# A tuned two-layer network kernel: leaking unit inside the MLP's products, shorter root chain, vector index from its known score, rounding in one piece

## Chip, cores and metric

One core of a Trainium2 chip. The metric is the device time in microseconds, the median of the runs. Engines: TensorE (PE, its weight loads PEld), VectorE (DVE), ScalarE (ACT), GpSimd (POOL), SyncE (SP, DMA issue).

## The reference

The input is `x` of 16 x 96 x 96 x 96 (images, channels, height, width). Two layers, each a mixing part and a feed-forward part with residuals:

```python
# layer 0
x = x + _L0_conv_ref(_ln_c(x), ...)
t = t + _L0_ffn_ref(_ln_t(t), W1, b1, W2, b2)      # t: x as tokens
# layer 1
x = x + _L1_conv_ref(_ln_c(x))                      # x / (2 + 1e-4 * 5x5 sum of squares) ** 0.75
t = t + _L1_ffn_ref(_ln_t(t), W1, b1, W2, b2)
```

The mixing part of layer 0 works on patches of 3 x 3 pixels. Each pixel is compared with 512 vectors; the best pair of pixel and vector is found, and an MLP makes the patch from it:

```python
y = einsum('ncij,vc->nvij', patches, w_mask) / (x_norm * w_norm)
idx = argmax(y.reshape(NL, -1))                     # max_ch, max_col = idx // 9, idx % 9
integrate = max_act * max_sim + w_mask[max_ch] * (1.0 - max_sim)
inp = concatenate([integrate, sim_map_max])         # 96 + 9
h = leaky_relu(inp @ w_i1.T + b_i1, 0.2)            # 288
vcs = tanh(h @ w_i2.T + b_i2)
h1 = relu(vcs @ w_l1.T + b_l1)
h2 = h1 @ w_l2.T + b_l2                             # then w_conv
```

The feed-forward parts (96 to 384 to 96) round their inputs, weights and hidden values to an 8-bit float (5 exponent, 2 mantissa bits) and sums to 16 bits.

## The kernel before

A tile is 128 patches (partitions) of J = 9 pixels and C = 96 channels; there are 128 tiles, 8 per image (`SLOTS`). The program is a software pipeline written by hand: each engine runs `steps(body)`, and in step k every part works on another tile (`PARTS`: `fs` loads and statistics, `f1` scores and selection, `f2` the search of the vector, `f3` the MLP, `back` and `tail` the feed-forward of layer 0, `pre` and `rear` layer 1). There are 145 steps; in the last ones only layer 1 is left. Engines run their bodies in the written order and wait for each other by semaphores, so the order of each body sets the order of the work.

What the change and the prediction touch, by the order in a step:

- Scores, TensorE `score` (L375, product L385) and VectorE `score_max` (L728, L731): nine 128x512 products go into two banks in turn, and VectorE takes the maximum over the 512 vectors of each (`mx`). Product j waits for maximum j-2 (`score_taken`).
- `mlp_input` (L778) on VectorE makes `inp` (96 + 9 columns) for the MLP. The links of `pixel_roots` (L707, `inverse_root` L688) go between: a seed by integer arithmetic (L692), the input times -0.5 (L693), then three rounds of three links (L697, L700, L703), each waiting for the one before by a semaphore, and the last instruction `nb1` (L717), which sets `root_ready`. GpSimd begins its step behind `root_ready` (L1067).
- The MLP: TensorE turns `inp` (L402), ScalarE copies it (`inpT`), `mlp_in` (L407) makes three 96x128 products, ScalarE adds the bias to each (`z1`, L596), VectorE makes the leaking unit in one instruction (`leaky`, L799: the larger of z and 0.2 z), and `mlp_mid` (L414) sums three products. Then tanh (L606), `mlp_last` (L420), `conv` (L428), `residual1` (L807).
- The vector: the chosen pixel (`win`, gathered by GpSimd, L968) is turned (L391), multiplied with all 512 vectors again (`win_scores`, L397), and `win_vector` (L768) takes the largest score (MAX8, L772) and its index (L775), with which GpSimd gathers the vector (`wrow`, L976) and multiplies it with the tile (L984, L986).
- `hidden` (L812) on VectorE: for each of three 128x1152 blocks of hidden values an addition of the bias with relu (L817), and a rounding to 8-bit precision on the 16-bit pattern (L823), once per block, in two pieces of a chain: block c is rounded after the addition of block c+1. `fill` on TensorE waits for all three (`hid_ready`, L367), then makes 27 products (L370). Links of other chains go between, by `run(between, 1)`.
- `select` (L736): similarity, its maximum and index, the row number `xrow` for the pixel's gather, a cast of the index to float (`jf`, L753), a mask of the nine columns (`pick`, L756), and two products with the mask that sum (L759, L761).
- `lrn_columns` (L835): once per image, a chain on 128x72 values with another `inverse_root`, its links between other instructions of two steps. The step that has most of it is called the LRN step here; it follows the step with the window sums (`window_sums`, L432). GpSimd's `keep_root2` waits for its end (`lrn_ready`) in that step.
- `moments` (L947) on GpSimd makes the roots' arguments from the statistics (`args_ready`); `gather_pixel` stands behind it.

```python
                scores(0, 2)
                if k.f3 is not None:
                    leaky(k.f3)
                scores(2, WIN_TURN)
                if k.fs is not None:
                    dve.wait_ge(xt_loaded[k.p], landed(k.fs, k.p))
                    last = group_stats(1, xt[:, k.fs & XT - 1], between)
                if k.f2 is not None:
                    win_vector(k.f2, between)
```

## Time and profile before

| | |
|---|---|
| median of 3 runs | 3665.52 us (3658.46 to 3670.87) |
| the profiled execution: time, span | 3659.15 us, 3657.4 us |
| instructions | 63346 |
| VectorE busy | 3093.2 us (85%), 11127 instructions |
| TensorE busy | 3038.1 us (83%), 17928 instructions |
| ScalarE busy | 2890.6 us (79%), 7558 instructions |
| GpSimd busy | 2569.9 us (70%), 3993 instructions |
| HBM | 52 GB/s over the span |
| mean granted TensorE clock | 0.945 |

Busy time is the union of an engine's instructions; records of one engine overlap a little. Idle time stands before the instruction that ended it, with the engine and the instruction that released it. The granted clock is a share of 2.4 GHz.

### The profile page before, as it was taken

Reading aid. Unit: us, or ns where it says so; the run is one execution under the profiler, and the core shown is the slowest. Engines: PE = TensorE matmul, PEld = TensorE weight load, DVE = VectorE, ACT = ScalarE, POOL = GpSimd, SP = SyncE. Lnnn points to the kernel's source line nnn. Section 1 sums busy time; section 2 is a strip of 40 time slices with the busy share of each in tenths; the row PEclk is TensorE's granted clock in tenths of the full one; section 3 lists DMA queues with packets and bytes.
Section 4 is the critical chain, followed back from the end, with each engine's and each line's share of the span. In section 5 each row is a group of like instructions: output and inputs, shape, how many; then the busy total and the mean of one; then the engine's idle time right before and its main releaser. Section 6 shows DMA issues by size and latency. Waiting matters only on the chain. (4 is left out here: it accounts for less than half of the span.)

```text
span 3657.4 us, 63346 instructions
## 1 busy us (share of the span) xinstructions
PE 3038.1 (83%) x17928; PEld 1674.1 (46%) x17928; DVE 3093.2 (85%) x11127; ACT 2890.6 (79%) x7558; POOL 2569.9 (70%) x3993
## 2 busy tenths in 40 slices
PE   5887888888888888888888888888888888888755
PEld 2444454444445444444444444444444444444332
DVE  6788989889888998889889888889998888999631
ACT  0444888878788887878878788888888888888877
POOL 2455677767777777777767777776777777777753
PEclk9999999999999999999999999999999999999855
DMA  3111111111111121111111111121211111111000
GB/s 84 45 37 45 46 60 54 60 50 56 58 55 60 50 65 50 57 58 55 60 50 57 58 55 55 55 65 50 60 55 56 59 50 61 54 59 46 23 30 34
DMA packets 64515, 195.70 MB, mean 54 GB/s; under 512 B 11392, under 2 KB 14633, under 8 KB 64169
## 3 DMA queue, kind: packets, MB, share of 16 engines
q1 hardware_dynamic: 53928, 172.76, 14.8%
q0 software_dynamic: 10240, 18.89, 2.1%
q8 instruction: 148, 2.42, 0.3%
q14 instruction: 199, 1.62, 0.1%
HBM read 134.60 MB, written 57.02 MB: 52 GB/s over the span
## 5 line engine op out<-in xcount | busy, mean ns | idle before, releaser
L385 PE MATMUL banks<-wcT,xc 128*128 128x512 f32 x2304 | 1217.4, 631 | 108.8 <-DVE mx L731 104.2
L518 ACT ACTIVATE ffn_hid<-banks 128x384 f16<-128x384 f32 x2304 | 1026.8, 487 | 296.5 <-PE banks L362 273.1
L731 DVE TENSOR_REDUCE mx<-banks 128x1 f32<-128x512 f32 x1152 | 774.7, 683 | 227.9 <-PE banks L385 218.4
L362 PE MATMUL banks<-ffn_xT,w1q 128*128 128x384 bf16 x2304 | 678.1, 348 | 177.4 <-ACT ffn_hid L518 138.3
L994 POOL TENSOR_TENSOR ffn_f<-ffn_y,b2q 128x864 f16<-128x864 f16 x256 | 469.7, 1835 | 375.5 <-DVE nb L717 300.1
L362 PEld LDWEIGHTS banks<-ffn_xT,w1q 128*128 128x128 bf16 x2304 | 228.7, 100 | 790.6 <-ACT ffn_hid L518 588.1
L385 PEld LDWEIGHTS banks<-wcT,xc 128*128 128x128 f32 x2304 | 422.6, 199 | 350.8 <-DVE mx L731 150.8
L817 DVE TENSOR_SCALAR ffn_hid<-ffn_hid,b1q 128x1152 f16<-128x1152 f16 x768 | 420.9, 559 | 126.1 <-ACT ffn_hid L518 126.0
L996 POOL TENSOR_TENSOR x<-x,ffn_f 128x864 f32<-128x864 f32 x256 | 488.3, 1907 | 20.1
L551 ACT ACTIVATE ffn_x<-x,cols 128x96 fp8e5<-128x96 f32 x1152 | 461.4, 456 | 0.0
L551 ACT ACTIVATE ffn_x<-x,nb,roots 128x96 fp8e5<-128x96 f32 x1152 | 424.9, 455 | 0.0
L724 DVE BATCH_NORM_STATS2 st<-x 128x6 f32<-128x96 f32 x2304 | 408.0, 245 | 8.9 <-POOL x L996 8.9
L984 POOL TENSOR_TENSOR prod_dot<-xt,wrow 128x864 f32<-128x864 f32 x128 | 271.0, 2117 | 200.3 <-DMA wrow<-vector_table,vidx 200.3
L428 PE MATMUL banks<-wc,h 128*128 128x480 f32 (+1 forms) x1024 | 393.2, 527 | 0.0
L518 ACT ACTIVATE ffn_xT<-banks 96x384 bf16<-96x384 f32 x768 | 345.1, 483 | 60.0 <-PE banks L355 40.2
L370 PEld LDWEIGHTS banks<-w2q,ffn_hid 128*128 128x128 f16 x6912 | 330.1, 101 | 127.2 <-issue 125.2
L518 ACT ACTIVATE ffn_y<-banks 128x480 f16<-128x480 f32 (+1 forms) x512 | 257.1, 531 | 163.4 <-PE banks L370 146.9
L370 PE MATMUL banks<-w2q,ffn_hid 128*128 128x96 bf16 x6912 | 351.8, 211 | 39.2 <-DVE ffn_hid L823 39.2
L355 PE MATMUL banks<-ident_b,ffn_x 128*96 128x128 bf16 x2304 | 228.1, 227 | 144.3 <-ACT ffn_xT L518 116.9
L823 DVE TENSOR_SCALAR ffn_hid<-ffn_hid 128x1152 uint16<-128x1152 uint16 x768 | 338.3, 452 | 0.0
L355 PEld LDWEIGHTS banks<-ident_b,ffn_x 128*96 128x96 fp8e5 x2304 | 177.9, 125 | 255.1 <-ACT ffn_xT L518 155.7
L564 ACT ACTIVATE x<-x,cols 128x96 f32<-128x96 f32 x640 | 293.3, 460 | 0.3 <-POOL cols L1004 0.3
(147 smaller groups left out, 4474.0 us busy)
## 6 DMA issues: line engine op xcount, KB each, us to landing
xt<-x_tok_in SPq DMA_DIRECT2D x128, 432.0 KB, 3.2
xc<-x_chan_in SPq DMA_DIRECT2D x128, 432.0 KB, 3.6
out_tok<-x SPq DMA_DIRECT2D x128, 432.0 KB, 2.5
win<-x_tok_in,xrow POOLq DMA_INDIRECT x128, 2.6
wrow<-vector_table,vidx POOLq DMA_INDIRECT x128, 2.7
shift<-shift_in SPq DMA_DIRECT2D x1, 960.0 KB, 5.7
vector_table<-wtab SPq DMA_DIRECT2D x1, 384.0 KB, 3.3
...
```

The lines of the kernel that those rows point to most:

```text
L355: last = pe.matmul(bank[0:C, i * P:(i + 1) * P], ffn.x8[:, u * G + i, :], ident_b[:, :], start=True, stop=True)
L362: last = pe.matmul(bank[:, 0:GW], w1q[:, ffn.layer, c * P:(c + 1) * P], ffn.xT[:, g * GW:(g + 1) * GW], start=True, stop=True)
L370: last = pe.matmul(bank[:, (j - j0) * C:(j - j0 + 1) * C], ffn.hid[:, c, j * P:(j + 1) * P], w2q[:, ffn.layer, c, :], start=(c == 0), stop ...
L385: last = pe.matmul(ps_score[score_bank(j)], xc[p][:, j, :], wcT[:, :], start=True, stop=True)
L428: last = pe.matmul(bank[:, 0:(j1 - j0) * C], h1[:, q, :], wc[:, q, j0 * C:j1 * C], start=(q == 0), stop=(q == 1))
L518: return nc.scalar.activation(dst, src, ACT.Copy)
L551: last = nc.scalar.activation(ffn.x8[:, j, :], x[:, j, :], ACT.Identity, bias=bias_c[:, j:j + 1], scale=scale_c[:, j:j + 1], saturate=False)
L724: last = nc.vector.bn_stats(st3[:, which, j, :], src[:, j, :])
L731: nc.vector.tensor_reduce(mx[p][:, j:j + 1], ps_score[score_bank(j)], AX.X, ALU.max).then_inc(score_taken, 1)
L817: nc.vector.tensor_scalar(ffn.hid[:, c, :], ffn.hid[:, c, :], b1q[:, ffn.layer, c:c + 1], 0.0, ALU.add, ALU.max).then_inc(ffn.rounded, 1)
L994: tt(ffn.f[:, :, :], ffn.y[:, :, :], b2, ALU.add).then_inc(ffn.f_ready, 1)
L996: tt(dst, x, ffn.f[:, :, :], ALU.add).then_inc(ready, 1)
```

## The change

1. The leaking unit is written as 0.2 z + 0.8 relu(z). The linear part, with the bias, goes through a matrix made once at the start (`leak`, from `wi1r` and `wi2`, times 0.2), as a fourth product of `mlp_mid` on `inpT`. `inp` gets a 106th column of ones, which carries the bias `b_i1`. ScalarE makes 0.8 relu(z) of all three blocks in one instruction, straight into `h`. `z1`, `z1_ready` and VectorE's `leaky` go.
2. `inverse_root` has a seed and seven links: one round with a polynomial of second degree (four links), one of Newton's (three). The multiplication by -0.5 beside the seed goes, since the factor sits in the first link of a round.
3. `select` compares `iota` with the index directly, without the cast, and a third product with the mask writes the raw score of the chosen pixel into `vtop`. `win_vector` looks for that score at once; its MAX8 and one link go.
4. `hidden` adds to all three blocks first and then rounds 128x3456 in one instruction; `hid_ready` is set once per tile.

```diff
@@ mlp_mid
                 pe.wait_ge(h_ready, f3 + 1)
+                pe.matmul(ps_a[0:C, 0:P], leak[:, :], inpT[:, :], start=True, stop=False)
                 for c in range(M1):
-                    last = pe.matmul(ps_a[0:C, 0:P], wi2[:, c, :], h[:, c, :], start=(c == 0), stop=(c == M1 - 1))
+                    last = pe.matmul(ps_a[0:C, 0:P], wi2[:, c, :], h[:, c, :], start=False, stop=(c == M1 - 1))
@@ scalar, body
                     act.wait_ge(z1_made, k.f3 + 1)
-                    for c in range(M1):
-                        last = nc.scalar.activation(z1[:, c * P:(c + 1) * P], ps_b[0:C, c * P:(c + 1) * P],
-                                                    ACT.Identity, bias=bmlp[:, c:c + 1])
-                    last.then_inc(z1_ready, 1)
+                    nc.scalar.activation(h[:].rearrange("c m p -> c (m p)"), ps_b[0:C, 0:M1 * P], ACT.Relu,
+                                         scale=1.0 - LEAK).then_inc(h_ready, 1)
@@ vector
-            root_links = 11
+            root_links = 8
...
-                chain.add(nc.vector.tensor_scalar(y.bitcast(i32), x.bitcast(i32), -0.5, ROOT_SEED, ALU.mult, ALU.add),
-                          nc.vector.tensor_scalar(xh, x, -0.5, None, ALU.mult))
-                yield
-                for _ in range(3):
+                chain.add(nc.vector.tensor_scalar(y.bitcast(i32), x.bitcast(i32), -0.5, ROOT_SEED, ALU.mult, ALU.add))
+                yield
+                for scale, inner, outer in ((ROOT_POLY[2] ** 0.5, ROOT_POLY[1] / ROOT_POLY[2] ** 0.5, ROOT_POLY[0]),
+                                            (-0.5, None, 1.5)):
                     chain.wait()
-                    chain.add(nc.vector.tensor_tensor(t, y, y, ALU.mult))
+                    chain.add(stt(out=t, in0=y, scalar=float(scale), in1=y, op0=ALU.mult, op1=ALU.mult))
                     yield
                     chain.wait()
-                    chain.add(nc.vector.tensor_tensor(t, t, xh, ALU.mult))
+                    chain.add(nc.vector.tensor_tensor(t, t, x, ALU.mult))
                     yield
+                    if inner is not None:
+                        chain.wait()
+                        chain.add(stt(out=t, in0=t, scalar=float(inner), in1=t, op0=ALU.add, op1=ALU.mult))
+                        yield
                     chain.wait()
-                    chain.add(nc.vector.scalar_tensor_tensor(out=y, in0=t, scalar=1.5, in1=y, op0=ALU.add,
-                                                             op1=ALU.mult))
+                    chain.add(stt(out=y, in0=t, scalar=float(outer), in1=y, op0=ALU.add, op1=ALU.mult))
                     yield
@@ select
-                f1c.add(nc.vector.tensor_copy(jf[:, :], jidx[:, 0:1]))
-                yield
-                f1c.wait()
-                f1c.add(nc.vector.tensor_scalar(pick[p][:, :], iota[:, :], jf[:, 0:1], None, ALU.is_equal))
+                f1c.add(nc.vector.tensor_tensor(pick[p][:, :], iota[:, :], jidx[:, 0:1].broadcast_to([P, J]),
+                                                ALU.is_equal))
...
+                nc.vector.scalar_tensor_tensor(out=junk[:, 2, :], in0=pick[p][:, :], scalar=1.0, in1=mx[p][:, :],
+                                               op0=ALU.mult, op1=ALU.mult,
+                                               accum_out=vtop[p][:, 0:1]).then_inc(pick_ready, 1)
@@ win_vector
                 dve.wait_ge(win_scored, f2 + 1)
-                f2c.begin(f2)
-                f2c.add(nc.vector.max(vtop[:, :], ps_score[0]))
-                next(between, None)
-                f2c.wait()
-                nc.vector.max_index(vidx[:, :], vtop[:, :], ps_score[0]).then_inc(vidx_ready, 1)
+                dve.wait_ge(pick_ready, f2 + 1)
+                nc.vector.max_index(vidx[:, :], vtop[q][:, :], ps_score[0]).then_inc(vidx_ready, 1)
@@ hidden
-                relu(0)
-                run(between, 1)
-                for c in range(1, HC):
+                for c in range(HC):
                     relu(c)
                     run(between, 1)
-                    round_up(c - 1)
-                    run(between, 1)
-                round_up(HC - 1)
+                dve.wait_ge(ffn.rounded, (tile + 1) * HC)
+                bits = ffn.hid[:, :, :].rearrange("p c n -> p (c n)").bitcast(U16)
+                nc.vector.tensor_scalar(bits, bits, TO_E5M2, TO_E5M2, ALU.add,
+                                        ALU.subtract).then_inc(ffn.hid_ready, 1)
+                run(between, 1)
@@ vector, body
                 scores(0, 2)
-                if k.f3 is not None:
-                    leaky(k.f3)
                 scores(2, WIN_TURN)
```

VectorE's order at the end of a step, where the hidden values of layer 0 are rounded with the selection between (`ffn_hid` the hidden values, `sim` to `junk` the selection). Before, up to the last rounding piece, behind which two products with the mask follow:

```order
L817 TENSOR_SCALAR ffn_hid<-ffn_hid,b1q 128x1152
L741 TENSOR_TENSOR sim<-mx,roots 128x9
L817 TENSOR_SCALAR ffn_hid<-ffn_hid,b1q 128x1152
L744 MAX top<-sim 128x8
L823 TENSOR_SCALAR ffn_hid<-ffn_hid 128x1152
L747 MAX_INDEX jidx<-top,sim 128x8
L817 TENSOR_SCALAR ffn_hid<-ffn_hid,b1q 128x1152
L751 TENSOR_TENSOR xrow<-jidx,row_base 128x1
L753 CAST jf<-jidx 128x1
L823 TENSOR_SCALAR ffn_hid<-ffn_hid 128x1152
L756 TENSOR_SCALAR pick<-iota,jf 128x9
L823 TENSOR_SCALAR ffn_hid<-ffn_hid 128x1152
```

With the change:

```order
L825 TENSOR_SCALAR ffn_hid<-ffn_hid,b1q 128x1152
L755 TENSOR_TENSOR sim<-mx,roots 128x9
L825 TENSOR_SCALAR ffn_hid<-ffn_hid,b1q 128x1152
L758 MAX top<-sim 128x8
L825 TENSOR_SCALAR ffn_hid<-ffn_hid,b1q 128x1152
L761 MAX_INDEX jidx<-top,sim 128x8
L833 TENSOR_SCALAR ffn_hid<-ffn_hid 128x3456
L765 TENSOR_TENSOR xrow<-jidx,row_base 128x1
L767 TENSOR_TENSOR pick<-iota,jidx 128x9
L771 SCALAR_TENSOR_TENSOR junk,wmean<-pick,mom 128x9
L773 SCALAR_TENSOR_TENSOR junk,wrstd<-pick,roots 128x9
L776 SCALAR_TENSOR_TENSOR junk,vtop<-pick,mx 128x9
```

Two of the three rounding instructions are gone and the one left is three times as wide; `xrow` stands behind it, and there is a third product with the mask.

VectorE's order behind the roots (`mx` the score maxima, `h` the leaking unit, `vtop` and `vidx` the search of the vector). Before:

```order
L731 TENSOR_REDUCE mx<-banks 128x1 x2
L799 SCALAR_TENSOR_TENSOR h<-z 96x384
L731 TENSOR_REDUCE mx<-banks 128x1 x2
L724 BN_STATS st<-xt 128x6 x9
L772 MAX vtop<-banks 128x8
L775 MAX_INDEX vidx<-vtop,banks 128x8
L731 TENSOR_REDUCE mx<-banks 128x1
```

With the change:

```order
L745 TENSOR_REDUCE mx<-banks 128x1 x4
L738 BN_STATS st<-xt 128x6 x9
L788 MAX_INDEX vidx<-vtop,banks 128x8
L745 TENSOR_REDUCE mx<-banks 128x1
L738 BN_STATS st<-x 128x6 x9
```

The leaking unit and the MAX are gone, the four maxima stand together.

TensorE's order around the MLP's middle product (`xc` the score products, `h` and `leak` the middle product, `winT` the chosen pixel's scores). Before:

```order
L385 MATMUL banks<-wcT,xc 128x512
L362 MATMUL banks<-ffn_xT,w1q 128x384 x2
L385 MATMUL banks<-wcT,xc 128x512
L414 MATMUL banks<-h,wi 96x128 x3
L362 MATMUL banks<-ffn_xT,w1q 128x384 x2
L420 MATMUL banks<-vcs,wl 72x128 x2
L397 MATMUL banks<-wcT,winT 128x512
```

With the change:

```order
L393 MATMUL banks<-wcT,xc 128x512
L370 MATMUL banks<-ffn_xT,w1q 128x384 x2
L393 MATMUL banks<-wcT,xc 128x512
L421 MATMUL banks<-inpT,leak 96x128
L423 MATMUL banks<-h,wi 96x128 x3
L370 MATMUL banks<-ffn_xT,w1q 128x384 x2
L429 MATMUL banks<-vcs,wl 72x128 x2
L405 MATMUL banks<-wcT,winT 128x512
```

One product on `inpT` is added ahead of the three.

## Rows read from the trace of the kernel before

**Rows 1.** The page's first part: busy time, share and instructions of each engine.

```profile
PE 3038.1 (83%) x17928; PEld 1674.1 (46%) x17928; DVE 3093.2 (85%) x11127; ACT 2890.6 (79%) x7558; POOL 2569.9 (70%) x3993
```

**Rows 2.** Windows: busy us of PE, PEld, DVE, ACT, POOL, granted clock, DMA.

```profile
1000.00:2000.00 1000.00, 861.95 (x5249) 477.19 (x5248) 892.20 (x3226) 844.59 (x2213) 748.65 (x1152) 0.98 0.18 57
...
1753.00:1757.00 4.00, 4.00 (x14) 1.87 (x12) 2.37 (x4) 1.23 (x3) 3.92 (x3) 0.66 0.00 0
```

**Rows 3.** Timeline, VectorE, ordinary step: start us, busy us, line, tiles, [idle before].

```profile
1890.29 0.59 DVE L785 TENSOR_REDUCE dots<-half_dot 128x9 f32<-128x432 f32 x1
...
1891.54 0.18 DVE L692 TENSOR_SCALAR roots<-args 128x36 int32<-128x36 int32 x1
1891.64 0.41 DVE L693 TENSOR_SCALAR rtmp<-args 128x36 f32<-128x36 f32 x1
...
1892.08 0.20 DVE L697 TENSOR_TENSOR rtmp<-roots 128x36 f32<-128x36 f32 x1
...
1894.14 0.17 DVE L717 SCALAR_TENSOR_TENSOR nb<-mom,roots 128x9 f32<-128x9 f32 x1
...
1895.43 1.20 DVE L799 SCALAR_TENSOR_TENSOR h<-z 96x384 f32<-96x384 f32 x1
...
1899.94 0.70 DVE L772 MAX8 vtop<-banks 128x8 f32<-128x512 f32 x1 [0.49 <-PE banks L397]
...
1909.70 0.69 DVE L731 TENSOR_REDUCE mx<-banks 128x1 f32<-128x512 f32 x1 [1.17 <-PE banks L385]
...
1915.64 0.59 DVE L785 TENSOR_REDUCE dots<-half_dot 128x9 f32<-128x432 f32 x1
```

**Rows 4.** Timeline of the same step, TensorE.

```profile
1892.12 0.36 PE L402 MATMUL banks<-ident,inp 128*105 128x128 f32 x1 [0.52 <-DVE inp L794]
...
1894.13 0.31 PE L391 MATMUL banks<-ident,win 128*96 128x128 f32 x1
1894.96 1.13 PE L385 MATMUL banks<-wcT,xc 128*128 128x512 f32 x2 [0.52 <-DVE mx L731]
...
1897.11 0.82 PE L414 MATMUL banks<-h,wi 96*96 96x128 f32 x6
```

**Rows 5.** Timeline of the same step, GpSimd.

```profile
1890.45 0.25 POOL L962 TENSOR_TENSOR args<-var,eps 128x27 f32<-128x27 f32 x1
...
1903.82 1.09 POOL L976 DMA_INDIRECT wrow<-vector_table,vidx  x1
...
1911.92 0.50 POOL L955 TENSOR_TENSOR mtmp<-st 128x27 f32<-128x27 f32 x2 [0.69 <-DVE st L724]
```

**Rows 6.** Groups of instructions, VectorE: the rounding pieces.

```profile
L823 DVE TENSOR_SCALAR ffn_hid<-ffn_hid 128x1152 uint16<-128x1152 uint16 x768 | 338.3, 452 | 0.0
```

**Rows 7.** Timeline of an LRN step: VectorE, then TensorE, then GpSimd.

```profile
1835.01 1.87 DVE L799 SCALAR_TENSOR_TENSOR h<-z 96x384 f32<-96x384 f32 x1 [1.15 <-ACT z L596]
...
1845.19 2.27 DVE L817 TENSOR_SCALAR ffn_hid<-ffn_hid,b1q 128x1152 f16<-128x1152 f16 x1
...
1837.03 0.87 PE L414 MATMUL banks<-h,wi 96*96 96x128 f32 x6 [0.85 <-DVE h L799]
...
1851.77 2.08 PE L385 MATMUL banks<-wcT,xc 128*128 128x512 f32 x2 [3.00 <-DVE mx L731]
...
1845.10 2.05 POOL L984 TENSOR_TENSOR prod_dot<-xt,wrow 128x864 f32<-128x864 f32 x1 [1.77 <-DMA wrow<-vector_table,vidx]
```

**Rows 8.** Timeline of the step behind it, TensorE.

```profile
1865.84 0.45 PE L391 MATMUL banks<-ident,win 128*96 128x128 f32 x1 [1.29 <-DMA win<-x_tok_in,xrow]
```

**Rows 9.** Timeline of a step of the drain, VectorE and TensorE.

```profile
3539.07 0.52 DVE L817 TENSOR_SCALAR ffn_hid<-ffn_hid,b1q 128x1152 f16<-128x1152 f16 x1 [0.87 <-ACT ffn_hid L518]
3539.50 0.82 DVE L823 TENSOR_SCALAR ffn_hid<-ffn_hid 128x1152 uint16<-128x1152 uint16 x2
...
3540.47 2.32 PE L370 MATMUL banks<-w2q,ffn_hid 128*128 128x96 bf16 x27 [1.97 <-DVE ffn_hid L823]
```

More of the change, by code:

```diff
@@ L42 @@
 HC = HID // P
-D1 = C + J
+D1 = C + J + 1
+LEAK = 0.2
 M1 = 3
@@ L61 @@
 ROOT_SEED = float(0x5F3759DF)
+ROOT_POLY = np.polynomial.Chebyshev.interpolate(
+    lambda w: w ** -0.5, 2, domain=[0.9324, 1.0691]).convert(kind=np.polynomial.Polynomial).coef
 LRN_POLY = np.polynomial.Chebyshev.interpolate(
@@ L132, in build @@
         wi2 = sb("wi2", [C, M1, C])
+        wi1r = sb("wi1r", [C, M1, D1])
+        leak = sb("leak", [D1, C])
         wl1 = sb("wl1", [C, 2 * LH])
@@ L136, in build @@
         wc = sb("wc", [P, 2, J * C])
-        bmlp = sb("bmlp", [C, M1 + 1 + 2])
+        bmlp = sb("bmlp", [C, 1 + 2])
         w1raw = sb("w1raw", [C, 2, HID])
@@ L164, in build @@
         roots = [sb(f"roots_{i}", [P, 4, J]) for i in range(2)]
-        rtmp = sb("rtmp", [P, 2, 4 * J])
+        rtmp = sb("rtmp", [P, 4 * J])
         nb1 = sb("nb1", [P, J])
@@ L177, in build @@
         winT = sb("winT", [P, P])
-        vtop = sb("vtop", [P, 8])
+        vtop = [sb(f"vtop_{i}", [P, 8]) for i in range(2)]
         vidx = sb("vidx", [P, 8], U32)
@@ L330, in _ @@
         def _(pe):
-            pe.wait_ge(w_loaded, 16 * 15)
+            pe.wait_ge(w_loaded, 16 * 16)
             pe.wait_ge(table_ready, 1)
@@ L341, in _ @@
                                      wconv[:, :], start=True, stop=True)
+            for c in range(M1):
+                last = pe.matmul(banks[0:D1, 5, 0:C], wi1r[:, c, :], wi2[:, c, :], start=(c == 0), stop=(c == M1 - 1))
             last.then_inc(w_pe, 1)
@@ L527, in _ @@
                 last = copy(wc[0:LH + q, q, 5 * C:J * C], banks[0:LH + q, 2 + 2 * q, 0:4 * C])
-            last.then_inc(w_act, 1)
+            nc.scalar.activation(leak[:, :], banks[0:D1, 5, 0:C], ACT.Copy, scale=LEAK).then_inc(w_act, 1)
             def take(ffn, tile, first, units):
@@ L648, in _ @@
             nc.vector.memset(st3[:], 0.0)
+            for v in vtop:
+                nc.vector.memset(v[:], 0.0)
             nc.vector.memset(h1[:], 1.0)
+            nc.vector.memset(inp[:], 1.0)
             nc.vector.memset(wc[:], 0.0)
@@ L714, in pixel_roots @@
                 y = flat(roots[k.p])
-                yield from inverse_root(rc, flat(args), y, rtmp[:, 0, :], rtmp[:, 1, :])
+                yield from inverse_root(rc, flat(args), y, rtmp[:, :])
                 rc.wait()
@@ L787, in mlp_input @@
                          nc.vector.tensor_scalar(mix[:, 1:2], top_q, -1.0, 1.0, ALU.mult, ALU.add))
-                f3c.add(nc.vector.tensor_tensor(inp[:, C:D1], dots[:, :], roots[q][:, 3, :], ALU.mult),
+                f3c.add(nc.vector.tensor_tensor(inp[:, C:C + J], dots[:, :], roots[q][:, 3, :], ALU.mult),
                         nc.vector.tensor_scalar(wnorm[:, :], win[q][:, :], wmean[q][:, 0:1], mix[:, 0:1],
@@ L795, in mlp_input @@
                                                in1=wnorm[:, :], op0=ALU.mult, op1=ALU.add).then_inc(inp_ready, 1)
-            def leaky(f2):
-                dve.wait_ge(z1_ready, f2 + 1)
-                nc.vector.scalar_tensor_tensor(out=h[:].rearrange("c m p -> c (m p)"), in0=z1[:, :], scalar=0.2,
-                                               in1=z1[:, :], op0=ALU.mult, op1=ALU.max).then_inc(h_ready, 1)
             def residual1(f2, q):
@@ L839, in lrn_columns @@
                 alpha, beta, rstd, bias = (flat(b) for b in cols_i)
-                w, t, rg, arg, xh = (lbuf[:, i, :] for i in range(5))
+                w, t, rg, arg = (lbuf[:, i, :] for i in range(4))
                 dve.wait_ge(box_made, n + 1)
@@ L874, in lrn_columns @@
                 lc.wait()
-                yield from inverse_root(lc, arg, rstd, t, xh)
+                yield from inverse_root(lc, arg, rstd, t)
                 lc.wait()
@@ L908, in body @@
                 if k.f2 is not None:
-                    win_vector(k.f2, between)
+                    win_vector(k.f2, k.q, between)
                 between = factors
@@ L1126, in layouts @@
     wl2 = np.concatenate([w["w_l2"].reshape(c32, J, 2 * LH), w["b_l2"].reshape(c32, J, 1)], 2)
-    bmlp = np.zeros((C, M1 + 3), np.float32)
-    bmlp[:, 0:M1] = w["b_i1"].reshape(M1, C).T
-    bmlp[:, M1] = w["b_i2"]
-    bmlp[0:LH, M1 + 1:] = w["b_l1"].reshape(2, LH).T
+    bmlp = np.zeros((C, 3), np.float32)
+    bmlp[:, 0] = w["b_i2"]
+    bmlp[0:LH, 1:] = w["b_l1"].reshape(2, LH).T
     both = lambda f: np.stack([f(a[f"L{i}_ffn_W1"], a[f"L{i}_ffn_b1"], a[f"L{i}_ffn_W2"], a[f"L{i}_ffn_b2"])
@@ L1136, in layouts @@
         "wm": w["w_mask"],
-        "wi1": w["w_i1"].T,
+        "wi1": np.concatenate([w["w_i1"].T, w["b_i1"][None]], 0),
+        "wi1r": np.concatenate([w["w_i1"], w["b_i1"][:, None]], 1).reshape(M1, C, D1).transpose(1, 0, 2),
         "wi2": w["w_i2"].T.reshape(M1, C, C).transpose(1, 0, 2),
```

40 lines of the change are left out of this document (17 added, 23 removed).

## The prediction

> **What bounds the kernel now.** I read the engine totals first. VectorE is busy for 85% of the span, TensorE for 83% [rows 1], and between 1000 and 2000 us for 89% and 86% [rows 2]. No engine is full, so a shorter VectorE pays only where TensorE waits for it, or where a loop of waits goes through it. So the next view is the timeline of one ordinary step, engine by engine.
>
> From one dots reduction to the next (1890.29 to 1915.64) an ordinary step lasts 25.35 us [rows 3]. It falls into two stretches.
>
> Stretch A goes from the eighth score maximum (1909.70) through the statistics, the rounding of layer 0, the selection, the MLP's input and the roots to the first two maxima of the next step, which end at 1895.43 (one step later, at 1920.8). The third score product starts after the first of them, having waited 0.52 us for it; the transpose of `inp` had waited 0.52 us as well [rows 4]. So VectorE sets the time in A, for 10.6 us (1909.70 to 1894.96 plus 25.35).
>
> Stretch B goes from that score product (1894.96) to 1909.70, 14.7 us. Here it is VectorE that waits: 0.49 us before the MAX8 and 1.17 us before the eighth maximum [rows 3]. TensorE and ScalarE hand banks to each other and set the pace. What VectorE saves in B is worth nothing unless TensorE waits for that very result.
>
> Once in eight steps VectorE also carries the 72-wide LRN chain. There, leaky waited 1.15 us for `z` and took 1.87 us, TensorE waited 0.85 us for `h`, a rounding step took 2.27 us beside the GpSimd product of 1845.10, and TensorE waited 3.00 us for a maximum [rows 7]. In the step behind it TensorE waited 1.29 us for the gathered pixel [rows 8], whose gather stands on GpSimd behind moments that had waited for the LRN chain.
>
> **The change, part by part.** *Roots.* Nine links run from 1892.08 to 1894.14, 0.23 us each [rows 3]; seven stay, so 0.46 us go. The multiplication by -0.5 beside the seed goes as well: it began 0.10 us after the seed and its 0.41 us ended at 1892.05, just ahead of the first link. That is worth 0.08 to 0.17, I take 0.13. Together 0.59 us in A. TensorE allows that much: it was free at 1894.44 (1894.13 + 0.31) and started at 1894.96 [rows 4], which leaves 0.52 us, and the transpose of `inp` comes 0.08 earlier because one instruction ahead of `inp` is gone. **-0.59 us** where A is VectorE's.
>
> *Rounding in one piece, selection.* One piece of 3456 has no row. Three pieces of 452 ns that overlap by some 0.08 us take about 1.1 us [rows 6]; one piece saves nothing at worst and two fixed parts at best. The smallest spacing between small instructions (seed to multiplication) is 0.10 us [rows 3], so it takes 0.9 to 1.1 us. I take 1.0. By the Trainium skill, "VectorE: DVE Perf Modes", section on the errata, an SBUF source costs 58 plus elements/4 cycles at 0.96 GHz, an estimate of 0.96 us. The 0.1 us is given back, since the piece must wait until the third addition has ended, where before an older piece filled that gap, and since the selection has a third accumulating product in place of the cast. Net 0, from -0.2 to +0.3. The row number `xrow` now comes behind the 1.0 us piece. Its gather stands behind the moments on GpSimd's queue (arguments ready at 1890.70, roots asked for them at 1891.54 [rows 3, 5]), so that delay is covered; without that cover it would be 1 us.
>
> *Leaking unit.* VectorE loses an instruction of about 1.2 us in B [rows 3], worth nothing in an ordinary step: TensorE took `h` at 1897.11 without a wait [rows 4]. ScalarE's three passes become one, in a place where it then waits for TensorE. TensorE gets one more product. Three such products (six instructions) take 0.82 us at 1897.11 [rows 4], at most 0.27 each; overlapped I take 0.25. B is TensorE's, nothing hides it: **+0.25 us** in all 128 steps.
>
> *Known score.* The MAX8 of 0.70 us goes, also in B [rows 3]. The index of the vector is ready up to 0.7 us earlier, yet its gather at 1903.82 stands in GpSimd's queue behind work that started with the roots [rows 5]. Worth 0.
>
> *The LRN step.* The wait for `h` goes: 0.85 us. VectorE no longer does leaky (1.87 with its 1.15 of waiting) nor MAX8, and three links less. The layer 1 rounding then begins about 1.4 us earlier against GpSimd's product. Two additions get in ahead of it; the third, and then the whole piece, wait for the product and the half sum behind it. I put the sixth maximum about 2.1 us earlier, so of the 3.00 us wait [rows 7] about 2 go, 0.66 of which are the earlier start. With the dropped link behind, about **-2.8 us** for the step, from -0.8 to -4. The third thing is the step behind it: `lrn_ready` is some 3 us earlier, the moments and the gather follow, and of the 1.29 us [rows 8] and the slow clock behind it I take **-1.2**, from 0 to -3.
>
> *Per image.* Of eight steps, six have A on VectorE (in the LRN step A is TensorE's behind the window products, in the one behind it the gather's): 6 x -0.59 = -3.5; 8 x +0.25 = +2.0; -2.8 and -1.2. That is -5.5 us, times 16 images **-88**.
>
> *Drain.* In the last steps only layer 1 is left. TensorE starts at 3540.47, 1.40 us behind the start of the third addition (3539.07) [rows 9]. Now it is 0.52 + 0.06 + 1.0 + 0.2 = 1.8, so +0.4 in 13 steps: **+5**.
>
> *Clock.* The granted clock is 0.98 between 1000 and 2000 us, so 4% of the time passes at 1.2 GHz instead of 2.4 GHz, and it was 0.66 in 1753 to 1757 [rows 2], behind the stretch with TensorE's waits. At twice the time for that work, 0.02 x 3300 = 66 us are lost. A shorter idle stretch should make some of these falls disappear; I take a quarter, **-15**, from +40 to -50.
>
> Sum: 3659 - 88 + 5 - 15 = 3561 us, against the profiled execution's 3659 (span 3657). The median shown is 3665.5, 6 higher, and the same offset gives **3567**. A measurement of this kernel can tell about 0.3% from no change, 11 us.
>
> **Rivals.** *TensorE takes it all back (slower).* Place: the third score product and `mlp_mid`. If its start in A is set by TensorE's own queue or by ScalarE's transposed pieces rather than by the roots, and the LRN step's wait only moves to GpSimd's products, then each step keeps the +0.25: 128 x 0.25 + 5 = +37, so 3703. It decides from the point where less than 0.25 us of the 0.59 gets through and the LRN steps give nothing. For it: TensorE's transposes for layer 1 and the MLP's first product, which wait for ScalarE, lie between the starts of 1892.12 and 1894.13; against it, two waits of 0.52 us are named for VectorE [rows 4]. Chance 0.11.
>
> *The rounding piece blocks GpSimd.* The rows show such blocking: 2.27 us for one addition beside a GpSimd product [rows 7]. A 1.0 us piece can hold up the issue at 1903.82 and the moments behind 1911.92. GpSimd has 0.69 us of waiting there [rows 5] and about 0.84 us between ready arguments (1890.70) and the roots. Two holds of 1.0 us exceed these 1.5 by 0.5: 6 x 16 x 0.5 = 48, and the LRN step loses half its gain (22): 3637. The Trainium skill states the mechanism, "SBUF — State Buffer", two separate sides: VectorE in a 2-port mode and GpSimd lock the shared pair for a whole instruction. Chance 0.15.
>
> *VectorE was the whole bound.* Then 0.59 + 1.2 + 0.7 = 2.5 us go per step, 128 x 2.5 = 320: 3345. Against it are VectorE's waits in B. Chance 0.04.
>
> *The clock falls away.* If nearly all low stretches go: 3567 - 35 = 3532, or with more gain in the LRN steps 3500. Chance 0.12. That the change does not do what it says I hold for excluded: the order shows the instructions gone, and a gather of another row would last as long.
>
> **How the numbers follow.** The forecast has 0.58, with its own range of 3515 to 3610. With the other cases, 3480 to 3640 leaves out the slower rival, the whole VectorE bound and a little of the edges, 0.2 in all. Faster 0.83; within 0.3% 0.06, half of it the edge of the blocked GpSimd; slower 0.11.
>
> **What would show it.** Right: dots to dots at 25.0 in an ordinary step; no or little wait before the third score product, with ScalarE named there if any; `mlp_mid` eight instructions, without a wait; VectorE's busy time down by about 350 us and its idle time up by 250; longer waits for the win scores and the eighth maximum; the LRN step at about 29 us instead of 31.6. Wrong: ordinary steps of 25.3 or more, GpSimd naming VectorE's rounding or the moments late at the roots, or TensorE's waits in A unchanged.

## The result, and the profile after

The changed kernel takes **3558.45 us** (median of 4 runs, 3554.84 to 3562.6) against 3666.67 for the kernel before in the same comparison: ratio **0.971**, 95% interval 0.969 to 0.973. Forecast: 3567 us, faster.

First the page, engine totals of the changed kernel:

```profile
PE 3011.0 (85%) x18190; PEld 1688.2 (48%) x18190; DVE 2778.1 (78%) x10043; ACT 2832.7 (80%) x7303; POOL 2566.0 (72%) x3993
```

VectorE lost 315 us of busy time against [rows 1], the span 104 us. The windows view answers to [rows 2] (busy us of PE, PEld, DVE, ACT, POOL, then the granted clock); the last row lies in an LRN step, behind TensorE's wait for a maximum:

```profile
1000.00:2000.00 1000.00, 881.79 (x5495) 499.17 (x5492) 824.25 (x3006) 854.86 (x2211) 774.59 (x1187) 0.99 0.18 58
...
1796.00:1800.00 4.00, 2.48 (x4) 1.09 (x5) 3.74 (x9) 0.04 (x1) 0.00 (x0) 0.66 0.00 0
```

One ordinary step on the timeline, VectorE (start us, busy us, line, tiles, [idle before <- releaser]), which answers to [rows 3]:

```profile
1880.73 0.59 DVE L798 TENSOR_REDUCE dots<-half_dot 128x9 f32<-128x432 f32 x1
...
1883.92 0.17 DVE L731 SCALAR_TENSOR_TENSOR nb<-mom,roots 128x9 f32<-128x9 f32 x1
1884.00 1.28 DVE L745 TENSOR_REDUCE mx<-banks 128x1 f32<-128x512 f32 x2
1885.90 0.69 DVE L745 TENSOR_REDUCE mx<-banks 128x1 f32<-128x512 f32 x1 [0.62 <-PE banks L393]
...
1899.70 0.69 DVE L745 TENSOR_REDUCE mx<-banks 128x1 f32<-128x512 f32 x1 [1.17 <-PE banks L393]
...
1904.02 1.03 DVE L833 TENSOR_SCALAR ffn_hid<-ffn_hid 128x3456 uint16<-128x3456 uint16 x1
1904.97 0.19 DVE L765 TENSOR_TENSOR xrow<-jidx,row_base 128x1 uint32<-128x1 uint32 x1
...
1905.60 0.59 DVE L798 TENSOR_REDUCE dots<-half_dot 128x9 f32<-128x432 f32 x1
```

The step is 24.87 us long, 0.48 shorter than in [rows 3]; `nb` comes 3.19 us behind the dots, where it came 3.85 behind. TensorE in the same step [rows 4]:

```profile
1882.45 0.32 PE L410 MATMUL banks<-ident,inp 128*106 128x128 f32 x1 [0.38 <-DVE inp L807]
...
1884.74 1.12 PE L393 MATMUL banks<-wcT,xc 128*128 128x512 f32 x2
...
1886.89 0.38 PE L421 MATMUL banks<-inpT,leak 106*96 106x128 f32 x2
1887.11 0.82 PE L423 MATMUL banks<-h,wi 96*96 96x128 f32 x6
```

The wait of 0.52 us before the third score product is gone and the leak product takes 0.22 us. Cut at three fixed places, the step before and after is:

| stretch of an ordinary step | before, us | after, us |
|---|---|---|
| eighth maximum to dots (statistics, rounding, selection) | 5.94 | 5.90 |
| dots to third score product (input, roots) | 4.67 | 4.01 |
| third score product to eighth maximum | 14.74 | 14.96 |

The gain sits in the second stretch, the leak product in the third. The LRN step, VectorE, TensorE, GpSimd [rows 7]:

```profile
1791.87 2.27 DVE L825 TENSOR_SCALAR ffn_hid<-ffn_hid,b1q 128x1152 f16<-128x1152 f16 x1
...
1795.68 1.04 DVE L833 TENSOR_SCALAR ffn_hid<-ffn_hid 128x3456 uint16<-128x3456 uint16 x1
...
1783.00 0.82 PE L423 MATMUL banks<-h,wi 96*96 96x128 f32 x6
...
1797.53 2.08 PE L393 MATMUL banks<-wcT,xc 128*128 128x512 f32 x2 [2.83 <-DVE mx L745]
...
1791.37 2.45 POOL L984 TENSOR_TENSOR prod_dot<-xt,wrow 128x864 f32<-128x864 f32 x1 [1.73 <-DMA wrow<-vector_table,vidx]
```

The wait for `h` is gone; the wait for a maximum is 2.83 us, where it was 3.00, and the clock falls behind it as before.

The new piece of 3456 does hold up GpSimd. One of the small instructions of `moments` falls beside it; before and after (busy us, mean ns):

```profile
L958 POOL TENSOR_TENSOR mtmp<-mtmp,quarter_c 128x27 f32<-128x27 f32 x133 | 61.7, 464 | 10.4
```

```profile
L958 POOL TENSOR_TENSOR mtmp<-mtmp,quarter_c 128x27 f32<-128x27 f32 x133 | 114.9, 864 | 10.4
```

Over all kernels of this document the mean is 0.43 to 0.47 us in the five with three pieces and 0.83 to 0.91 in the nine with one. It cost no time in an ordinary step: the roots' arguments end 0.65 us behind the start of the dots instead of 0.41, and VectorE asks for them at 1.26, so the prediction's rival of a blocked GpSimd had the mechanism right and not the price.

Where the gain came from, over the whole run: TensorE's score products by group, before and after (busy us, mean ns | idle before them, and for what).

```profile
L385 PE MATMUL banks<-wcT,xc 128*128 128x512 f32 x2304 | 1217.4, 631 | 108.8 <-DVE mx L731 104.2 <-ACT wc L518 2.4 <-DVE vidx L775 1.8
```

```profile
L393 PE MATMUL banks<-wcT,xc 128*128 128x512 f32 x2304 | 1187.8, 618 | 50.2 <-DVE mx L745 43.4 <-ACT leak L537 2.5 <-DVE vidx L788 1.0
```

TensorE waited 61 us less for maxima, nearly all of it outside the LRN steps: there 58.3 us became 2.2, in the 16 LRN steps 45.9 became 41.2. Its stretches at 1.2 GHz between 150 and 3300 us, counted in the trace's record of the granted clock, were 36 with 167 us in all, and are 20 with 89 us. At half the clock that is up to 39 us of lost time that did not occur.

### The profile page after: what moved, and what is told of

Read it like the earlier page. It is cut to its first block and busy times, and to the rows that moved or that the text cites. A ratio compares the mean times of both kernels' runs of the same rounds, so it can differ in the third digit from the quotient of the medians.

```text
span 3553.0 us, 62660 instructions
## 1 busy us (share of the span) xinstructions
PE 3011.0 (85%) x18190; PEld 1688.2 (48%) x18190; DVE 2778.1 (78%) x10043; ACT 2832.7 (80%) x7303; POOL 2566.0 (72%) x3993
## 5 line engine op out<-in xcount | busy, mean ns | idle before, releaser
L393 PE MATMUL banks<-wcT,xc 128*128 128x512 f32 x2304 | 1187.8, 618 | 50.2 <-DVE mx L745 43.4
L370 PE MATMUL banks<-ffn_xT,w1q 128*128 128x384 bf16 x2304 | 668.8, 343 | 177.3 <-ACT ffn_hid L527 138.0
L393 PEld LDWEIGHTS banks<-wcT,xc 128*128 128x128 f32 x2304 | 414.5, 196 | 282.8 <-issue 140.8
L825 DVE TENSOR_SCALAR ffn_hid<-ffn_hid,b1q 128x1152 f16<-128x1152 f16 x768 | 405.8, 551 | 139.0 <-ACT ffn_hid L527 138.6
L996 POOL TENSOR_TENSOR x<-x,ffn_f 128x864 f32<-128x864 f32 x256 | 466.6, 1823 | 20.1
L984 POOL TENSOR_TENSOR prod_dot<-xt,wrow 128x864 f32<-128x864 f32 x128 | 263.3, 2057 | 195.4 <-DMA wrow<-vector_table,vidx 195.4
L833 DVE TENSOR_SCALAR ffn_hid<-ffn_hid 128x3456 uint16<-128x3456 uint16 x256 | 270.5, 1057 | 4.0
```

The lines of the kernel that those rows point to most:

```text
L370: last = pe.matmul(bank[:, 0:GW], w1q[:, ffn.layer, c * P:(c + 1) * P], ffn.xT[:, g * GW:(g + 1) * GW], start=True, stop=True)
L393: last = pe.matmul(ps_score[score_bank(j)], xc[p][:, j, :], wcT[:, :], start=True, stop=True)
L825: nc.vector.tensor_scalar(ffn.hid[:, c, :], ffn.hid[:, c, :], b1q[:, ffn.layer, c:c + 1], 0.0, ALU.add, ALU.max).then_inc(ffn.rounded, 1)
L996: tt(dst, x, ffn.f[:, :, :], ALU.add).then_inc(ready, 1)
```

## The experiments

All are compared with the kernel before in the same set of runs. Four such sets were made, on three chips that are identified (the p runs, the u, m and `r_after` runs, and `b_best`). The kernel before took 3669, 3643, 3645 and 3672 us in them; the changed kernel took 3558.5 in its first comparison, whose chip is not recorded, and 3559.1 in the third set. So for the u runs I use times against `r_after`, measured on the same chip, and differences of a few us stay uncertain. "Step" is dots to dots, the commonest length of an ordinary step. Columns: ratio with 95% interval; ordinary step; mean LRN step and mean time per image over 12 images (from the third on); low clock between 150 and 3300 us.

| run | us | ratio | step | LRN | image | low clock us |
|---|---|---|---|---|---|---|
| before | 3666.67 | 1 | 25.36 | 31.8 | 214.2 | 167 |
| after | 3558.45 | 0.971 (0.969 to 0.973) | 24.87 | 30.4 | 207.0 | 89 |
| `r_after` | 3559.12 | 0.977 (0.974 to 0.980) | 24.85 | 30.6 | 207.0 | 89 |
| `p1_leak` | 3649.18 | 0.994 (0.992 to 0.996) | 25.58 | 31.3 | 212.9 | 106 |
| `p2_roots` | 3690.93 | 1.006 (1.004 to 1.008) | 26.29 | 31.0 | 216.1 | 116 |
| `p3_score` | 3620.54 | 0.986 (0.983 to 0.989) | 25.27 | 31.9 | 211.3 | 96 |
| `p4_round` | 3738.58 | 1.017 (1.013 to 1.021) | 25.57, 27.2 | 31.7 | 218.2 | 307 |
| `u1_leak` | 3552.05 | 0.974 (0.972 to 0.977) | 24.64 | 30.9 | 206.7 | 106 |
| `u2_roots` | 3649.72 | 1.002 (1.001 to 1.004) | 25.40 | 31.2 | 213.0 | 123 |
| `u3_score` | 3583.63 | 0.984 (0.982 to 0.985) | 25.08 | 30.8 | 208.6 | 92 |
| `u4_round` | 3552.12 | 0.975 (0.973 to 0.976) | 24.96 | 30.6 | 207.1 | 92 |
| `m2_lrn` | 3565.56 | 0.979 (0.976 to 0.982) | 24.85 | 28.9 | 207.4 | 96 |
| `m3_mask` | 3541.95 | 0.972 (0.969 to 0.975) | 24.57 | 30.0 | 206.2 | 99 |
| `b_best` | 4022.36 | 1.096 (1.092 to 1.100) | 26.4 to 30.6 | 34.0 | 239.7 | 420 |

**One part alone (p) and one part undone (u).** A p run is the kernel before with one part of the change, a u run the changed kernel without it. The diffs show the part as p adds it and u takes it back.

*Leaking unit.*

```diff
+                pe.matmul(ps_a[0:C, 0:P], leak[:, :], inpT[:, :], start=True, stop=False)
-                    for c in range(M1):
-                        last = nc.scalar.activation(z1[:, c * P:(c + 1) * P], ...)
+                    nc.scalar.activation(h[:]..., ps_b[0:C, 0:M1 * P], ACT.Relu, scale=1.0 - LEAK)
-                if k.f3 is not None:
-                    leaky(k.f3)
```

Expected of `p1_leak`: 

> The kernel before with the leaking unit folded into the products alone. Theory A (only what lies in stretch A, or what TensorE waits for in the LRN step, counts): the leaking instruction lay in B, where VectorE waits for TensorE; the extra product costs 0.22 us in each of 128 steps (+28 us), the LRN step's wait of 0.85 us for h goes (-14 us). So +5 to +20 us, 3672 to 3687. Theory B (VectorE's busy time counts wherever it lies, in proportion): of the 108 us this part has 1.2 of some 2.8 us per step, -46 us, 3620.

Expected of `u1_leak`: 

> The changed kernel with the leak put back on VectorE (z1 evicted by three ScalarE instructions, leaky on VectorE, no leak product); roots in eight links, known score and rounding in one piece kept. Theory C, the parts lean on each other: with the leaky unit on VectorE, the shorter roots bring VectorE to it before ScalarE has made z1, as in p2_roots, and it runs beside GpSimd's product, so most of the gain goes: 3620 to 3680 us, ordinary step 25.4 to 26.0, leaky waiting 0.5 us or more. Theory S, the parts add and each undoing costs what the part gave alone (17 us): 3572 to 3580 us, ordinary step 25.1 or less.

Measured: step 25.58 against 25.36 alone, and 24.64 against 24.85 undone. Alone the kernel is 20 us faster all the same, between the two theories: TensorE no longer waits for `h`, and the low clock fell from 167 to 106 us. The product costs 0.22 us in every ordinary step, whatever stands around it. Undone, the LRN step is 0.3 longer, the image 0.3 shorter, and the kernel 7 us faster than `r_after`: in this change the part is worth nothing, or slightly less. Theory C, which held the leaky unit for the partner of the roots, fell, and the measured time lies below theory S's range too.

*Roots.*

```diff
-            root_links = 11
+            root_links = 8
-                for _ in range(3):
+                for scale, inner, outer in ((ROOT_POLY[2] ** 0.5, ...), (-0.5, None, 1.5)):
```

Expected of `p2_roots`: 

> The kernel before with the root chain of a seed and seven links alone. Theory A: 0.5 to 0.6 us less in stretch A of the six steps per image in which VectorE sets it, and three links less in the LRN step: -50 to -65 us, 3602 to 3617, ordinary steps at 24.8. Theory B: 0.6 of 2.8 us per step, -23 us, 3643.

Expected of `u2_roots`: 

> The changed kernel with the roots in eleven links again. Theory C: without the leaky unit behind them the long roots cost their three links and one more instruction, 0.8 us of VectorE's busy time a step, of which 0.3 to 0.6 us lengthens the dots-to-dots step: 3590 to 3635 us. Theory S, the parts add: the short roots alone cost 21 us, so undoing them gives 3530 to 3545 us.

Measured: alone 0.6% **slower**, its step 0.93 us longer; undone 91 us slower than `r_after`. Of that, 0.55 us is in an ordinary step, inside theory C's 0.3 to 0.6; the time is above its 3590 to 3635 us, and the low clock rose from 89 to 123 us. Theory S fell. Nearly the whole gain of the change goes with this part. Without the short roots TensorE waits 100.5 us for maxima, with them alone in `p2_roots` 45.6. But in `p2_roots` the third score product comes only 0.17 us earlier behind the dots (4.51 instead of 4.67), and the stretch behind it is 1.10 longer (15.84 instead of 14.74). Why stands in the same step of `p2_roots`, VectorE, ScalarE, TensorE and GpSimd:

```profile
1901.65 1.98 DVE L806 SCALAR_TENSOR_TENSOR h<-z 96x384 f32<-96x384 f32 x1 [1.04 <-ACT z L599]
...
1896.90 0.57 ACT L521 ACTIVATE ffn_y<-banks 128x480 f16<-128x480 f32 x1 [0.53 <-PE banks L373]
1898.18 0.49 ACT L521 ACTIVATE ffn_y<-banks 128x384 f16<-128x384 f32 x1 [0.71 <-PE banks L373]
...
1899.61 0.37 PE L358 MATMUL banks<-ident_b,ffn_x 128*96 128x128 bf16 x3 [1.14 <-ACT ffn_xT L521]
...
1903.77 0.87 PE L417 MATMUL banks<-h,wi 96*96 96x128 f32 x6 [0.95 <-DVE h L806]
...
1901.39 1.82 POOL L1003 TENSOR_TENSOR x<-x,ffn_f 128x864 f32<-128x864 f32 x1
```

`nb` is earlier, so GpSimd starts its products earlier. ScalarE's second copy of `ffn_y` came 0.71 us late, and what stands behind it on ScalarE too: TensorE waited 1.14 us for `ffn_xT` ahead of the third score product (0.41 in `u1_leak`), which used up most of the 0.6 us that VectorE had gained, and `z` is late. Leaky, with two SBUF operands, starts at 1901.65 inside a product of GpSimd that ends at 1903.21, and ends 0.42 behind that end. In the kernel before, leaky's 1.20 us at 1895.43 [rows 3] also ended 0.42 behind the end of a product (1896.21), but that was the first product of the step; here leaky just missed its end (1901.31) and met the second. By group, over the run, `p2_roots` then `u1_leak`, which has the same leaky and the same short roots:

```profile
L806 DVE SCALAR_TENSOR_TENSOR h<-z 96x384 f32<-96x384 f32 x128 | 226.7, 1771 | 131.7 <-ACT z L599 131.4
...
L417 PE MATMUL banks<-h,wi 96*96 96x128 f32 x768 | 112.5, 284 | 94.2 <-DVE h L806 94.2
```

```profile
L806 DVE SCALAR_TENSOR_TENSOR h<-z 96x384 f32<-96x384 f32 x128 | 117.0, 914 | 58.4 <-ACT z L598 58.4
...
L416 PE MATMUL banks<-h,wi 96*96 96x128 f32 x768 | 106.8, 275 | 14.3 <-DVE h L806 14.3
```

TensorE's 94 us of waiting for `h` is 0.74 us a step (15.5 us over the run in the kernel before), most of what the step of `p2_roots` lost. In `u1_leak` `z` was ready before the first product ended: leaky ran from 1852.76 to 1853.56, that product to 1853.15. The late copy by itself does not lengthen a step: `p1_leak` has it too (74.2 us in all), and its step is longer by the leak product's 0.22 alone. That leaky and the product met because of both, the late copy and the early `nb`, is read from these traces; no run takes one of them away. The late copy remains unexplained: the wait before ScalarE's second copy is 70.4 us over `p2_roots` and 5.9 over the kernel before; it is there in most steps of `p1_leak` (0.67), `p2_roots` and `p3_score` (0.25) and not in the other kernels, though TensorE's 27 products are recorded at the same pace.

*Known score.*

```diff
-                f1c.add(nc.vector.tensor_copy(jf[:, :], jidx[:, 0:1]))
-                f2c.add(nc.vector.max(vtop[:, :], ps_score[0]))
+                nc.vector.scalar_tensor_tensor(out=junk[:, 2, :], ..., accum_out=vtop[p][:, 0:1])
```

Expected of `p3_score`: 

> The kernel before with the known score (no MAX8, no cast) alone. Theory A: MAX8 lay in B, so 0 in ordinary steps and up to 0.7 us in the LRN step: 0 to -12 us, 3655 to 3667. Theory B: 0.7 of 2.8 us per step, -27 us, 3639.

Expected of `u3_score`: 

> The changed kernel with the index cast and MAX8 back (vector found by searching its score). Theory C: MAX8 lies on the way to the vector's index in the second half of the step and the cast ahead of the masks at its end: 0.1 to 0.3 us a step, 3570 to 3600 us. Theory S: alone this part gave 46 us, nearly all by fewer stretches at the low clock; undone it costs the same, 3600 to 3610 us, and the low stretches between 150 and 3300 us rise from 89 us towards 160.

Measured: alone 48 us (1.4%), more than either theory allowed, with a step only 0.09 shorter, so most of it by fewer stretches at the low clock (96 us of them against 167). Undone it costs 24.5 us against `r_after`, as theory C had it, and there the step is 0.23 longer while the low clock is the same. From the end of the selection of `u3_score`:

```profile
1893.22 0.20 DVE L764 TENSOR_TENSOR xrow<-jidx,row_base 128x1 uint32<-128x1 uint32 x1
1893.34 0.14 DVE L766 CAST jf<-jidx 128x1 f32<-128x1 uint32 x1
...
1894.01 0.59 DVE L798 TENSOR_REDUCE dots<-half_dot 128x9 f32<-128x432 f32 x1
```

From `xrow` to the dots 0.79 us, in the changed kernel 0.63 (1904.97 to 1905.60). Behind a rounding in one piece nothing covers the cast's link any more, and 0.16 of the 0.23 us are that. MAX8 costs an ordinary step nothing: the stretch in which it stands, third score product to eighth maximum, is 14.96 us in `u3_score` and in the changed kernel, and 14.74 in `p3_score` and in the kernel before.

*Rounding in one piece.*

```diff
-                    round_up(c - 1)
...
+                dve.wait_ge(ffn.rounded, (tile + 1) * HC)
+                bits = ffn.hid[:, :, :].rearrange("p c n -> p (c n)").bitcast(U16)
```

Expected of `p4_round`: 

> The kernel before with the rounding in one piece alone. Theory A: nothing in ordinary steps (the piece waits for the third addition), +5 us in the drain: 3660 to 3675. Theory B: 0.3 of 2.8 us per step, -11 us, 3655.

Expected of `u4_round`: 

> The changed kernel with the rounding again in three pieces between the RELUs. Theory C: the piece cost 72 us alone because it held the masks and the scan of maxima back until TensorE fell silent and its clock dropped in every second step; in the changed kernel it sits in a step that has slack, so undoing it is worth -15 to +15 us: 3543 to 3575 us, ordinary step 24.7 to 25.0, low stretches as in the changed kernel or fewer. Theory S: undoing it gives 72 us back, 3480 to 3500 us.

Measured: alone 1.7% **slower**, outside both theories; undone, as theory C had it, 7 us faster than `r_after` (step 0.1 longer, step with the window sums 26.51 instead of 26.89). `p4_round`, TensorE and then the windows:

```profile
1756.42 0.36 PE L405 MATMUL banks<-ident,inp 128*105 128x128 f32 x1 [0.74 <-DVE inp L797]
...
1759.26 2.04 PE L388 MATMUL banks<-wcT,xc 128*128 128x512 f32 x2 [0.58 <-DVE mx L734]
```

```profile
1756.00:1760.00 4.00, 2.59 (x18) 1.92 (x19) 3.66 (x15) 3.36 (x11) 1.67 (x2) 0.92 0.07 14
1760.00:1764.00 4.00, 4.00 (x14) 1.96 (x12) 2.31 (x4) 1.27 (x4) 3.92 (x3) 0.66 0.00 0
```

With the wait for `inp` at 0.74 us (0.52 before) and that for the maximum at 0.58, the clock falls in every second step or more: 68 stretches against 36, and each such step lasts 27.2 us instead of 25.57. A delay of 0.2 us costs 1.65 here. A long wait for `inp` alone does not do it: in `u3_score` it is 0.60 us in an ordinary step and the low clock is that of the changed kernel, but there the next wait, for the maximum ahead of the third score product, is 0.06. The three kernels of the table in which that second wait is 0.5 us or more (the kernel before, `u2_roots`, `p4_round`) have 167, 123 and 307 us of low clock; the others but `b_best` have 89 to 116.

The four parts alone sum to +24 us against the 3669 of their set; together they give -108. **They do not add.** The undoings sum to +101 us, 91 of them the roots, against 86 for the whole change on that chip: nearer, but no sum either.

**Two edits to the changed kernel, and its repeat.** Expected of `r_after`: 

> The changed kernel once more, as the partner of the two runs beside it and of the undoings. All theories: 0.971 of the kernel before, within 0.003; ordinary step 24.87, window step 26.93, LRN step 29.8 to 30.8, low stretches between 150 and 3300 us around 90 us.

It came out as the first time (3559.12 us, step 24.85); the ratio, 0.977, misses the expected 0.971 by more than the 0.003 allowed, because the kernel before was 22 us faster on that chip.

`m2_lrn` in the LRN step:

```diff
+                if early:
+                    scores(5, 7, 1)
+                    if k.f3 is not None:
+                        residual1(k.f3, k.q)
                 if k.rear is not None:
                     hidden(ffn1, k.rear, between)
```

Expected: 

> The changed kernel; in the 16 LRN steps VectorE takes the maxima of scores 5 and 6 and the residual ahead of the hidden pieces of the second FFN instead of behind them. Theory V, the LRN step is set by where VectorE reaches those maxima (TensorE waits 2.83 us for one at 1797.53 and falls to the low clock): LRN step shorter by 1.5 to 2.8 us, 24 to 45 us in all, and the low stretches behind it gone, 3500 to 3535 us. Theory N, its length is the factors' own chain with the pieces between its links (GpSimd waited 6.29 us for it at 1801.38): the step keeps its length within 0.5 us and the time is that of the changed kernel within 8 us, or longer where TensorE then waits for the hidden pieces.

Measured: theory V is right on the step and wrong on the time. LRN step 28.9 instead of 30.6. The step behind it takes 26.2 to 28.1 us in nine of the 16 images and 24.8 to 25.1 in the last six; over the 12 images its mean is 26.7 instead of 24.9. In all 6 us slower. `m2_lrn`, TensorE behind the LRN step, and the windows:

```profile
1395.70 1.31 PE L378 MATMUL banks<-w2q,ffn_hid 128*128 128x96 bf16 x27 [1.73 <-DVE ffn_hid L833]
1397.82 0.46 PE L410 MATMUL banks<-ident,inp 128*106 128x128 f32 x1 [0.80 <-DVE inp L807]
```

```profile
1394.00:1396.00 2.00, 0.30 (x8) 0.33 (x8) 1.97 (x10) 0.00 (x0) 1.81 (x4) 1.00 0.02 4
...
1398.00:1404.00 6.00, 5.75 (x22) 3.87 (x22) 3.12 (x10) 3.30 (x9) 4.49 (x4) 0.50 0.04 8
```

The wait for a maximum turned into one for the rounded hidden values at the end of the step, and where the clock falls behind it, 6 us at half clock in this image, the step gives back more than the 1.6 us won.

`m3_mask`:

```diff
                 scores(0, 2)
+                if k.f2 is not None:
+                    masked(k.q)
                 scores(2, WIN_TURN)
```

Expected: 

> The changed kernel; the pick and its three masked products go from the end of the step to behind the second maximum of the next. Theory V, the dots come when VectorE's chain at the step's end lets them: dots, the input and the roots come 0.5 us earlier, and the ordinary step shortens by 0.2 to 0.5 us in 96 and more steps: 3510 to 3540 us. Theory N, the end of the step waits for the last score product and half_dot, and the start of the next pays the 0.7 us back where VectorE had waited: step within 0.1 us, 3550 to 3565 us on the chip of the first comparison.

Measured: step 24.57, 17 us **faster** than `r_after`, the fastest of all: theory V on the step, 2 us above its range in time. The pick and the three products no longer stand ahead of the dots, which come 5.39 us behind the eighth maximum instead of 5.88; 0.29 of these 0.5 us reach the step, since TensorE then waits 0.95 us for ScalarE's `ffn_xT`. What they cost at their new place, VectorE and then GpSimd:

```profile
1878.32 0.82 DVE L770 TENSOR_TENSOR pick<-iota,jidx 128x9 f32<-128x9 f32 x1
...
1879.26 1.79 DVE L775 SCALAR_TENSOR_TENSOR junk<-pick,roots 128x9 f32<-128x9 f32 x1
1880.98 0.08 DVE L775 DVE_READ_ACCUMULATOR junk<-pick,roots 128x1 f32 x1
...
1877.29 1.82 POOL L997 TENSOR_TENSOR ffn_f<-ffn_y,b2q 128x864 f16<-128x864 f16 x1 [0.88 <-DVE nb L731]
1879.18 1.84 POOL L999 TENSOR_TENSOR x<-x,ffn_f 128x864 f32<-128x864 f32 x1
```

An instruction on nine columns, 0.16 us at its old place, takes 1.79 us and ends where GpSimd's product does (1881.02). VectorE had that time to give: its waits at the next two maxima (0.62 and 0.49 in the changed kernel) are gone, and TensorE waits for neither.

Then the two gains together, `b_best` (`u1_leak` with the masks moved behind leaky):

```diff
                     leaky(k.f3)
+                if k.f2 is not None:
+                    masked(k.q)
```

Expected: 

> The two edits that made the changed kernel faster, together: the leaky unit back on VectorE (no leak product) and the pick with its masked products behind it, after the second maximum. Theory A, the gains are of two engines and add: ordinary step 24.87 - 0.23 - 0.30 = 24.34, time 3525 to 3538 us. Theory L, both put instructions with two SBUF operands beside GpSimd's products, where m3_mask had one of 128x9 last 1.79 us, until the product of GpSimd ended: leaky and the masked products then stretch to 3 us and more, the next maxima come late and TensorE waits for them again: step 24.6 or more and 3540 us or more, no better than m3_mask.

Measured: 4022 us, 9.6% slower than the kernel before. VectorE, TensorE, GpSimd:

```profile
1381.73 2.19 DVE L807 SCALAR_TENSOR_TENSOR h<-z 96x384 f32<-96x384 f32 x1 [0.82 <-ACT z L598]
1383.85 1.77 DVE L764 TENSOR_TENSOR pick<-iota,jidx 128x9 f32<-128x9 f32 x1
...
1385.75 1.79 DVE L769 SCALAR_TENSOR_TENSOR junk<-pick,roots 128x9 f32<-128x9 f32 x1
...
1388.39 1.28 PE L399 MATMUL banks<-wcT,winT 128*128 128x512 f32 x2 [2.33 <-DVE mx L739]
...
1383.47 2.13 POOL L998 TENSOR_TENSOR ffn_f<-ffn_y,b2q 128x864 f16<-128x864 f16 x1
```

Three instructions in turn each wait out a product of GpSimd, 5.8 us from 1381.73 to 1387.54; the two small ones took 0.16 us each at their old place. TensorE then waits 2.33 us for the next maximum, and the clock follows (420 us at the low clock). Theory L had the mechanism; its "3 us and more" was too little by half, and it did not have the clock. The Trainium skill, "SBUF — State Buffer", section "Who interferes with whom", states the lock: a VectorE instruction with two SBUF inputs and a GpSimd instruction that reads SBUF exclude each other for the whole instruction. These rows agree, down to 128x9.

## Why the prediction was right, point by point

- **Roots, -0.59 in A.** Right, and the term that carries the change: undone, the step is 0.55 longer, and the wait of 0.52 us before the third score product is gone. `nb` comes 0.66 earlier.
- **Leak product, +0.25.** 0.22, in both directions. That leaky was worth nothing in an ordinary step is right for this pair of kernels; `p2_roots` and `b_best` show that it is a risk kept out of GpSimd's products.
- **Rounding piece and selection, 1.0 us, net 0.** 1.03 to 1.06 us, and the stretch with both is 5.90 us instead of 5.94. The net is right for the two parts together only: the piece alone adds 0.2 us to the step (+70 us, the clock made 1.65 out of 0.2 in about every second step), in part because it uncovers the cast's link, which the known score takes away.
- **Known score, 0.** MAX8 is worth 0 in an ordinary step, as foretold. The cast is not: undone, 24.5 us, 0.16 us a step of it the uncovered link. The prediction set the cast off against the third accumulating product, but that follows the second without a link.
- **Ordinary step.** -0.49 measured, -0.34 by the sum. Of the missing 0.15, 0.04 is in the selection and 0.11 between dots and third score product, where the short roots' own share is 0.55: with the long roots but the other parts in (`u2_roots`) that stretch is 4.56 us instead of 4.67 already. There the multiplication by -0.5 takes 0.18 us instead of the 0.41 of [rows 3], and the first link starts 0.12 earlier. Why it was slow in the kernel before stays open.
- **LRN step, -2.8 + 0.25.** Mis-sized: -1.4. The wait for `h` went, as foretold, but of the 3.00 us wait for the maximum only 0.17 went, not 2. The sixth maximum starts 20.85 us behind the step's dots instead of 22.27, 1.42 earlier and not 2.1: the additions still fell beside GpSimd's product (2.27 us), and the piece behind them held the maximum until 1796.79. TensorE, rid of its wait for `h`, arrives 1.24 us earlier itself, and so waits as long as before. `m2_lrn` shows that even 1.6 us won there would mostly not have stayed.
- **Step behind it, -1.2.** The mean fell by 1.2 us (26.2 to 25.0), so the number came out, but not as argued: [rows 8] is of a step that 2 of the 16 images have (30.0 us), two more were at 25.7 and 26.9, and most were 25.2 us already and are 24.9 to 25.2.
- **Clock, a quarter of 66 us.** Half: 167 to 89 us of low clock, up to 39 us instead of 15. Of the 72 steps in the 12 images that are neither window nor LRN steps, 17 lasted over a us more than the common one before, and none does after.
- **VectorE's totals.** Busy -315 us, foretold -350; idle +211 (564 to 775), foretold +250.
- **Drain, +5.** TensorE's wait there is 2.32 us instead of the 1.97 of [rows 9], in ten steps and not 13, so 3.5 us.
- **GpSimd blocked by the piece, chance 0.15.** The blocking is there, one instruction of 0.46 us stretched to 0.86, and slack of the kind that the prediction counted (1.5 us) covered it.

Per image 7.2 us were measured. The sum has 5.5, and 6.4 with its clock term. Its LRN term was too large by about 1.2 us an image; the terms of the ordinary steps (0.15 us each) and of the clock were too small by more. That the total came within 9 us of the forecast is in part luck: these errors have opposite signs.
